# A GNN kernel whose degree histogram is laid out as 64 low columns by 98 spans instead of 128 by 49

## The chip, the cores and the metric

One NeuronCore of a Trainium2 chip runs the whole kernel. The metric is device time in microseconds (us) per execution. Engines are named as in the profile: PE is TensorE (PEld its weight loads), DVE is VectorE, ACT is ScalarE, POOL is GpSimd, SP is SyncE.

## What is computed

A graph of N = 6250 nodes and E = 100000 edges (src, dst), sorted by dst, with node features x of 6250x512 in float32. Cut to what matters:

```python
def reference(x, src, dst, ...):
    # layer 0: graph convolution with self loops
    deg  = segment_sum(ones, dst) + 1            # how many edges end in each node
    norm = rsqrt(deg)[src] * rsqrt(deg)[dst]
    h    = segment_sum(norm * (x @ W0)[src], dst) + b0 + t_emb @ Wt + bt
    x    = layernorm(x + h)
    # layers 1 and 2: mean over the incoming edges
    cnt  = segment_sum(ones, dst)
    h    = relu((segment_sum(x[src], dst) / max(cnt, 1)) @ Wl1.T + x @ Wr1.T + b1)
    h    = (segment_sum(h[src], dst) / max(cnt, 1)) @ Wl2.T + h @ Wr2.T + b2
    return layernorm(x + h)
```

All three layers need the number of edges that end in each node. That count is the histogram of this case.

## The kernel before, in words

**The constants.** P = 128 partitions, T = 49 tiles of 128 nodes, H = 64, WT = 98 windows of 64 nodes (two a tile), EC = 782 edges to a partition, HB = 34 edge columns to a block of the histogram, so EC / HB = 23 blocks.

**The histogram.** It is the first thing that the engines do, and nothing of the layers starts before it is done. SP loads dst into `dst_nat` (128x782, int32; L282). DVE makes from it `dst_hi` = dst >> 7 (the tile, 0 to 48; L473 and the cast L475), `dst_lo` = dst & 127 (the place in the tile; L474 and L478), and, for another purpose, `own_win` = dst >> 6 (the window, 0 to 97; L476, L479) and `next_win` of the next edge (L477, L480), from which L482 and L483 find whether the edges are sorted. POOL makes `iota_lo` (L378), in which element (v, c) is v.

Then for each block of 34 edge columns DVE writes two arrays of bfloat16 zeros and ones with one comparison each: `oh_lo`, 128 values by 34 columns (L494), and `oh_hi`, 49 values by 34 columns (L495). The column index c is the innermost, so the value index v has a step of 34 elements, 68 bytes. PE then runs 34 matmuls (L928), one for each column c: the stationary operand (the weights) is `oh_lo[:, half, :, c]`, 128 partitions by 128 columns, the moving one is `oh_hi[:, half, :, c]`, 128 partitions by 49 columns. Both are read with the step of 68 bytes. Each adds 128 edges to the counts in PSUM, `hist_ps[low, tile]` (`hist_ps` is another name for `root_ps`, which is how the profile writes it). L908 clears the bank before, and L937, a matmul of zeros, closes the sum and signals `hist_done`.

**What orders the two engines.** `oh_lo` and `oh_hi` have two halves. DVE waits on `oh_used` (L491) until PE has finished the block two before; PE waits on `oh_ready` (L926) for the block's arrays. The loop holds two blocks; the 23rd stands behind it.

**Behind the histogram.** DVE copies the counts (`cnt`, L504, 128x49), makes `rcnt` and `dinv` = 1 / sqrt(deg) (L505 to L509, with ACT), and 98 window totals by two matmuls of 64 partitions each (L942: `cnt[0:64]` is the first window of each tile, `cnt[64:128]` the second). From these come the tables that tell where windows end (L515 to L577). ACT and DVE scale x by `dinv` into `stage` (L793, L622), SP stores it as `table0` (L344), and when that is stored POOL starts the gathers (L441). SP's loads of dst rows, src rows and small weights behind `hist_done` (L316 to L327) go on beside that.

**The three layers.** POOL gathers 256 source rows a group by two indirect DMAs (L441) into a ring of 10 slots; PE adds them to the windows by matmuls with one-hot arrays (L1024), transposes a finished tile (L1007) and multiplies it by the weights (L1017); the root term is L1034. 391 groups a layer, three layers.

```python
            def one_hots(b, half):
                dve.wait_ge(S["oh_used"], b + 1)
...
                v.tensor_tensor(oh_lo[:, half, :, :], iota_lo[:, :, :], lo_b, ALU.is_equal)
                v.tensor_tensor(oh_hi[:, half, :, :], iota_lo[:, 0:T, :], hi_b,
                                ALU.is_equal).then_inc(S["oh_ready"], 1)
```

Of the kernel before, what the change touches and what calls it, by code (L numbers as in the profile page):

```python
# [5 lines left out]
def gnn_resnorm(nc, x, src, dst, t_emb, w0, b0, wt, bt, wl1t, wr1t, b1, wl2t, wr2t, b2, out):  # L6
    fp32, bf16 = mybir.dt.float32, mybir.dt.bfloat16
    i32, i16 = mybir.dt.int32, mybir.dt.int16
    ALU, ACT = mybir.AluOpType, mybir.ActivationFunctionType
# [3 lines left out]
    P = 128  # L13
    T = -(-N // P)
# [4 lines left out]
    H = P // 2  # L19
    WT = 2 * T  # L20
# [25 lines left out]
    EC = -(-E // P)  # L46
# [3 lines left out]
    HB = 34  # L50
# [6 lines left out]
    with ctx:  # L57
        def sb(name, shape, dt, scope=ctx):
            return scope.enter_context(nc.sbuf_tensor(name, shape, dt))
# [29 lines left out]
        zeros = sb("zeros", [P, P], bf16)  # L89
# [9 lines left out]

        early = ExitStack()  # L100
        dst_nat = sb("dst_nat", [P, EC], i32, early)
        dst_hi_i = sb("dst_hi_i", [P, EC], i32, early)
        dst_lo_i = sb("dst_lo_i", [P, EC], i32, early)
        dst_hi = sb("dst_hi", [P, EC], bf16, early)
        dst_lo = sb("dst_lo", [P, EC], bf16, early)
        iota_lo = sb("iota_lo", [P, P, HB], bf16, early)
        oh_lo = sb("oh_lo", [P, 2, P, HB], bf16, early)
        oh_hi = sb("oh_hi", [P, 2, T, HB], bf16, early)
        dst_next = sb("dst_next", [P, EC], i32, early)
        own_win_i = sb("own_win_i", [P, EC], i32, early)  # L110
        next_win_i = sb("next_win_i", [P, EC], i32, early)
        own_win = sb("own_win", [P, EC], bf16, early)
# [12 lines left out]
        cnt = sb("cnt", [P, T], fp32, mid)  # L125
# [60 lines left out]
        hist_ps = root_ps  # L186
# [188 lines left out]
        def _(pool):  # L375
            nc.gpsimd.memset(hpad[0:1, :], -1).then_inc(S["pad_made"], 1)
            nc.gpsimd.memset(X[:, T - 1, :], 0.0).then_inc(S["x_tail_zero"], 1)
            nc.gpsimd.iota(iota_lo[:, :, :], [[1, P], [0, HB]], base=0, channel_multiplier=0,  # L378
                           allow_small_or_imprecise_dtypes=True)
            nc.gpsimd.memset(zeros[:, :], 0.0)  # L380
            nc.gpsimd.memset(ones[:, :], 1.0)
# [73 lines left out]
        def _(dve):  # L455
            v = nc.vector
            count = [0]

            def link(ins):

                count[0] += 1
                ins.then_inc(S["chain"], 1)
                dve.wait_ge(S["chain"], count[0])
# [6 lines left out]
            dve.sem_inc(S["rstd_ready"], LAG)  # L470

            dve.wait_ge(S["dst_loaded"], 16 * 8)
            v.tensor_scalar(dst_hi_i[:, :], dst_nat[:, :], 7, None, ALU.arith_shift_right)  # L473
            link(v.tensor_scalar(dst_lo_i[:, :], dst_nat[:, :], P - 1, None, ALU.bitwise_and))  # L474
            v.tensor_copy(dst_hi[:, :], dst_hi_i[:, :])  # L475
            v.tensor_scalar(own_win_i[:, :], dst_nat[:, :], 6, None, ALU.arith_shift_right)  # L476
            v.tensor_scalar(next_win_i[:, :], dst_next[:, :], 6, None, ALU.arith_shift_right)  # L477
            link(v.tensor_copy(dst_lo[:, :], dst_lo_i[:, :]))  # L478
# [10 lines left out]
            def one_hots(b, half):  # L489

                dve.wait_ge(S["oh_used"], b + 1)  # L491
                lo_b = dst_lo[:, bass.ds(b * HB, HB)].unsqueeze(1).to_broadcast([P, P, HB])
                hi_b = dst_hi[:, bass.ds(b * HB, HB)].unsqueeze(1).to_broadcast([P, T, HB])
                v.tensor_tensor(oh_lo[:, half, :, :], iota_lo[:, :, :], lo_b, ALU.is_equal)  # L494
                v.tensor_tensor(oh_hi[:, half, :, :], iota_lo[:, 0:T, :], hi_b,  # L495
                                ALU.is_equal).then_inc(S["oh_ready"], 1)

            with dve.Fori(0, EC // HB - 1, 2) as b:
                one_hots(b, 0)
                one_hots(b + 1, 1)  # L500
            one_hots(EC // HB - 1, 0)
            dve.wait_ge(S["hist_done"], 1)
            dve.wait_ge(S["edges_copied"], 6 * 16)
            link(v.tensor_copy(cnt[:, :], hist_ps[:, 0:T]))  # L504
            link(v.tensor_scalar(rcnt[:, :], cnt[:, :], 1.0, None, ALU.max))  # L505
            v.tensor_scalar(dinv[:, :], cnt[:, :], 1.0, None, ALU.add).then_inc(S["deg_made"], 1)
            link(v.reciprocal(rcnt[:, :], rcnt[:, :]))
# [108 lines left out]
            for n, (first, many) in enumerate(TWOS):  # L616
                b = first // BT
                if b >= 2 and first % BT == 0:
                    dve.wait_ge((S["stage_stored0"], S["stage_stored1"])[b % 2], 16 * PAIRS * (b // 2))
                if many == 2:  # L620
                    t = first + 1
# [281 lines left out]
        def _(pe):  # L903
            mm = nc.tensor.matmul

            def clear(bank, cols):

                return mm(bank[:, 0:cols], zeros[:, :], zeros[:, 0:1].to_broadcast([P, cols]), start=True, stop=False,  # L908
                          skip_group_check=True)
# [9 lines left out]
            pe.wait_ge(S["consts_made"], 2)  # L919
            pe.wait_ge(S["order_read"], 1)  # L920
            mm(aggT_ps[0:1, 0:1], fall_sum[:, :], ones[:, 0:1], start=True, stop=True).then_inc(S["order_ps"], 1)
            clear(hist_ps, T)

            def count(b, half):

                pe.wait_ge(S["oh_ready"], b + 1)  # L926
                for c in range(HB):
                    last = mm(hist_ps[:, 0:T], oh_lo[:, half, :, c], oh_hi[:, half, :, c], start=False, stop=False,  # L928
                              skip_group_check=True)
                last.then_inc(S["oh_used"], 1)  # L930

            with pe.Fori(0, EC // HB - 1, 2) as b:
                count(b, 0)
                count(b + 1, 1)
            count(EC // HB - 1, 0)

            mm(hist_ps[:, 0:T], zeros[:, :], zeros[:, 0:T], start=False, stop=True,  # L937
               skip_group_check=True).then_inc(S["hist_done"], 1)

            pe.wait_ge(S["deg_made"], 1)  # L940
# [31 lines left out]
            for rows, banks, done in ((src_f, tmp_ps[0:2], "src_ps"), (drow_f, tmp_ps[2:4], "dst_ps")):  # L972
                for q in range(QC):
                    last = nc.tensor.transpose(banks[q // 4][:, q % 4 * CQ:(q % 4 + 1) * CQ], rows[0:CQ, q, :],
                                               ident[0:CQ, 0:CQ])
# [133 lines left out]
def build(nc, arrays):  # L1109
    args = [nc.dram_tensor(f"in_{n}", arrays[f"in_{n}"].shape, mybir.dt.from_np(arrays[f"in_{n}"].dtype),  # L1110
                           kind="ExternalInput").ap() for n in _INS]
    out = nc.dram_tensor("out_0", arrays["in_x"].shape, mybir.dt.float32, kind="ExternalOutput").ap()
    gnn_resnorm(nc, *args, out)
# [14 lines left out]
```

## Time and profile before

| | |
|---|---|
| median of 3 runs | 3257.88 us (3256.55 to 3260.6) |
| the profiled execution | 3249.74 us |
| its span on the core | 3248.0 us |
| mean granted TensorE clock | 0.932 of full |
| busy: PE, PEld | 2715.4 us (84%), 920.1 us (28%) |
| busy: DVE, ACT, POOL | 1075.9 us (33%), 493.5 us (15%), 2240.1 us (69%) |
| histogram, first matmul to last | 18.16 to 96.56 us |
| first gather | 140.91 us |

The profile is of one execution. The time of an execution is its span and some 1.7 us around it. Busy time of PE is the union of its matmuls, whose ends are modelled; "idle before" names what an engine waited for. A row's mean is of one instruction. In a timeline a row merges neighbouring instructions of one kind; it gives the start, the time from that start to the end of the last, and how many there are.

### The profile page before, as it was taken

To read this page: it belongs to the slowest core of one execution; us is meant where nothing else is said; L and a number is where in the kernel's file an instruction comes from. 1 tells how busy PE (TensorE), PEld (TensorE's weight loads), DVE (VectorE), ACT (ScalarE), POOL (GpSimd) and SP (SyncE) were. 2 spreads that over 40 slices of the span, in tenths; PEclk is the share of its full clock that TensorE was granted. 3 is DMA by queue.
4 is the path that set the end of the run, shared out by engine and by line. 5 is a ranking of instruction groups with operands and counts; after the bars stand their busy time and mean duration, and the time that the engine had idled before them with its cause. 6 is when DMAs were issued, how large, how long until landed. Compare 5 with 4: busy or idle time off the path is not lost.

```text
span 3248.0 us, 48588 instructions
## 1 busy us (share of the span) xinstructions
PE 2715.4 (84%) x9664; PEld 920.1 (28%) x9665; DVE 1075.9 (33%) x2322; ACT 493.5 (15%) x1044; POOL 2240.1 (69%) x2367
## 2 busy tenths in 40 slices
PE   7466677778898989899889888988888988888897
PEld 6211111222222233333322222223333333222222
DVE  8401122334454521122222233332222333333443
ACT  0200001111122210111111111120001111112222
POOL 1277777777777657777777777737777777777663
PEclk9766888999999999999999999999999999999999
DMA  6777777777777667778888887758777777777773
GB/s 197 255 210 209 209 216 220 223 222 228 225 229 229 197 189 242 235 236 252 247 244 248 248 248 240 243 175 249 238 227 230 240 232 230 234 219 229 207 212 120
DMA packets 255898, 729.72 MB, mean 225 GB/s; under 512 B 50026, under 2 KB 51596, under 8 KB 255842
## 3 DMA queue, kind: packets, MB, share of 16 engines
q0 software_dynamic: 187680, 615.14, 64.6%
q1 hardware_dynamic: 52528, 85.56, 7.4%
q10 hardware_dynamic: 15666, 28.72, 2.6%
q8 instruction: 12, 0.20, 0.0%
q14 instruction: 12, 0.10, 0.0%
HBM read 676.34 MB, written 53.71 MB: 225 GB/s over the span
## 4 chain that ended last, share of the span: by engine, by line
PE 59%; issue 15%; POOL 10%; DMA 7%; DVE 4%; DVEq 3%; ACT 2%; SPq 0%; POOLq 0%; ACTq 0%
PE sum_ps L1024 32%; PE prod_ps L1017 13%; PE root_ps L1034 10%; POOL raw L441 10%; DMA raw<-table,idx_ring 5%; PE aggT_ps L1007 2%; PE root_ps L928 1%; PE selfT_ps L1048 1%; ACT half_sum L825 1%; DMA raw<-rows,idx_ring 1%; DVE oh L720 1%; DVEq L254 1%; DVE X L641 1%; DVE X L644 1%; DMA selfbuf<-rows 1%
## 5 line engine op out<-in xcount | busy, mean ns | idle before, releaser
L441 POOL DMA_INDIRECT raw<-rows,idx_ring x1564 | 1487.1, 951 | 594.1 <-issue 501.0
L1024 PE MATMUL sum_ps<-raw,oh 128*64 128x512 f32 x4692 | 1228.1, 646 | 338.9 <-DMA raw<-table,idx_ring 153.5
L441 POOL DMA_INDIRECT raw<-table,idx_ring x782 | 742.7, 950 | 286.5 <-issue 259.5
L1017 PE MATMUL prod_ps<-W,aggT 128*128 128x512 f32 x1176 | 619.7, 652 | 28.2 <-issue 25.7
L1024 PEld LDWEIGHTS sum_ps<-raw,oh 128*64 128x64 f32 x4692 | 305.5, 142 | 1057.7 <-issue 1054.2
L671 DVE TENSOR_TENSOR agg<-sum_ps,half_sum 64x512 f32<-64x512 f32 x294 | 200.9, 683 | 1115.4 <-ACT half_sum L825 1115.2
L1034 PE MATMUL root_ps<-W,selfT 128*128 128x512 f32 x800 | 396.9, 642 | 103.4 <-issue 45.1
L825 ACT ACTIVATE half_sum<-sum_ps 64x512 f32<-64x512 f32 x294 | 174.4, 593 | 1231.5 <-PE sum_ps L1024 1231.5
L1017 PEld LDWEIGHTS prod_ps<-W,aggT 128*128 128x128 f32 x1176 | 213.6, 202 | 449.5 <-issue 449.5
L1024 PE MATMUL sum_ps<-raw,oh_next 128*64 128x512 f32 x1176 | 319.8, 622 | 9.4 <-DVE agg L671 9.4
L720 DVE TENSOR_TENSOR oh<-iota_ps,dst_rel 128x640 f32<-128x640 f32 x237 | 194.6, 821 | 382.5 <-PE sum_ps L1024 353.6
L1034 PEld LDWEIGHTS root_ps<-W,selfT 128*128 128x128 f32 x800 | 153.8, 202 | 333.7 <-issue 311.4
L699 DVE TENSOR_SCALAR oh_next<-iota_row,win_base,dst_end 128x64 f32<-128x64 bf16 x588 | 164.1, 334 | 44.3 <-DVE dst_end L696 18.7
L696 DVE CAST dst_end<-dst_tab 128x2 f32 x294 | 58.3, 198 | 361.7 <-issue 217.7
L836 ACT ACTIVATE selfT<-selfT_ps 128x512 f32<-128x512 f32 x100 | 59.7, 597 | 722.5 <-PE selfT_ps L1048 722.5
L815 ACT ACTIVATE aggT<-aggT_ps 128x512 f32<-128x512 f32 x147 | 87.9, 598 | 470.6 <-PE aggT_ps L1007 470.6
L1024 PEld LDWEIGHTS sum_ps<-raw,oh_next 128*64 128x64 f32 x1176 | 59.0, 136 | 243.2 <-issue 243.2
L1007 PE MATMUL aggT_ps<-ident,agg 128*128 128x128 f32 x588 | 96.8, 287 | 0.0
L1007 PEld LDWEIGHTS aggT_ps<-ident,agg 128*128 128x128 f32 x588 | 61.9, 141 | 120.7 <-issue 100.4
L928 PE MATMUL root_ps<-oh_hi,oh_lo 128*128 128x49 bf16 x782 | 75.0, 269 | 7.0 <-DVE oh_hi L495 6.8
L928 PEld LDWEIGHTS root_ps<-oh_hi,oh_lo 128*128 128x128 bf16 x782 | 70.3, 142 | 11.7 <-DVE oh_hi L495 11.7
L843 ACT ACTIVATE junk<-X,sums 128x512 f32 (+1 forms) x98 | 69.8, 712 | 6.5 <-DVE sums L663 6.5
(140 smaller groups left out, 761.9 us busy)
## 6 DMA issues: line engine op xcount, KB each, us to landing
selfbuf<-rows ACTq DMA_DIRECT2D x103, 256.0 KB
raw<-rows,idx_ring POOLq DMA_INDIRECT x1564, 3.8
rows<-X SPq DMA_DIRECT2D x49, 256.0 KB, 3.8
rows<-hbuf SPq DMA_DIRECT2D x49, 256.0 KB
X<-rows SPq DMA_DIRECT2D x49, 256.0 KB
raw<-table,idx_ring POOLq DMA_INDIRECT x782, 3.7
X<-in_x SPq DMA_DIRECT2D x6, 2048.0 KB
out<-X SPq DMA_DIRECT2D x48, 256.0 KB
```

Of the source, the lines that this page charges most:

```text
L441: nc.gpsimd.indirect_dma_start(out=raw[:, n, j, :], out_offset=None, in_=tables[L][:, :], in_offset=bass.IndirectOffsetOnAxis(ap=idx_ring[ ...
L671: v.tensor_tensor(agg[h * H:(h + 1) * H, :], sum_ps[0:H, :], half_sum[:, :], ALU.add).then_inc(S["agg_ready"], 1)
L699: made = v.tensor_scalar(oh_next[:, j, :], iota_row[:, 0:H], win_base[:, bass.ds(w1, 1)], dst_end[:, j:j + 1], ALU.add, ALU.is_equal)
L720: v.tensor_tensor(oh[:, which * HR:(which + 1) * HR, :, :].rearrange("p n j e -> p (n j) e"), iota_ps[:, 0:H].unsqueeze(1).to_broadcast([P ...
L815: a.activation(aggT[:, :], aggT_ps[:, :], ACT.Copy).then_inc(S["aggT_ready"], 1)
L825: a.activation(half_sum[:, :], sum_ps[H:P, :], ACT.Copy).then_inc(S["half_taken"], 1)
L843: a.activation(junk[:, :], tile_of_x(t1), ACT.Square, bias=column(sums, t1), accum_out=column(sqsum, t1)).then_inc(S["squares_made"], 1)
L928: last = mm(hist_ps[:, 0:T], oh_lo[:, half, :, c], oh_hi[:, half, :, c], start=False, stop=False, skip_group_check=True)
L1007: last = nc.tensor.transpose(aggT_ps[:, k * P:(k + 1) * P], agg[:, k * P:(k + 1) * P], ident[:, :])
L1017: last = mm(product(L, t1), aggT[:, k * P:(k + 1) * P], W[:, 0, k, :], start=(k == 0), stop=(k == KD - 1))
L1024: return mm(sum_ps[j * H:(j + 1) * H, :], of[:, j, :], raw[:, n, j, :], start=fresh, stop=False, skip_group_check=True)
L1034: last = mm(out_ps, xT[:, k * P:(k + 1) * P], W[:, n, k, :], start=(k == 0), stop=(k == KD - 1))
```

## The change

The node number is split at bit 6 in place of bit 7. `dst_lo` = dst & 63 has 64 values, and the other half of the split is `own_win` = dst >> 6 with 98 values, which DVE has anyway, so `dst_hi_i` and `dst_hi` go. The stationary operand is now 128 partitions by 64 columns and the moving one 128 by 98; the counts stand in PSUM as `hist_ps[0:64, 98]`. `cnt` keeps its layout: it is put together by two copies, one for even windows into partitions 0 to 63 and one for odd windows into 64 to 127, each reading every second column. The number of blocks, of matmuls (782) and the waits stay as they were.

```diff
-        dst_hi_i = sb("dst_hi_i", [P, EC], i32, early)
-        dst_hi = sb("dst_hi", [P, EC], bf16, early)
-        iota_lo = sb("iota_lo", [P, P, HB], bf16, early)
-        oh_lo = sb("oh_lo", [P, 2, P, HB], bf16, early)
-        oh_hi = sb("oh_hi", [P, 2, T, HB], bf16, early)
+        iota_lo = sb("iota_lo", [P, WT, HB], bf16, early)
+        oh_lo = sb("oh_lo", [P, 2, H, HB], bf16, early)
+        oh_hi = sb("oh_hi", [P, 2, WT, HB], bf16, early)
...
-            nc.gpsimd.iota(iota_lo[:, :, :], [[1, P], [0, HB]], base=0, channel_multiplier=0,
+            nc.gpsimd.iota(iota_lo[:, :, :], [[1, WT], [0, HB]], base=0, channel_multiplier=0,
...
-            v.tensor_scalar(dst_hi_i[:, :], dst_nat[:, :], 7, None, ALU.arith_shift_right)
-            link(v.tensor_scalar(dst_lo_i[:, :], dst_nat[:, :], P - 1, None, ALU.bitwise_and))
-            v.tensor_copy(dst_hi[:, :], dst_hi_i[:, :])
+            link(v.tensor_scalar(dst_lo_i[:, :], dst_nat[:, :], H - 1, None, ALU.bitwise_and))
...
-                lo_b = dst_lo[:, bass.ds(b * HB, HB)].unsqueeze(1).to_broadcast([P, P, HB])
-                hi_b = dst_hi[:, bass.ds(b * HB, HB)].unsqueeze(1).to_broadcast([P, T, HB])
-                v.tensor_tensor(oh_lo[:, half, :, :], iota_lo[:, :, :], lo_b, ALU.is_equal)
-                v.tensor_tensor(oh_hi[:, half, :, :], iota_lo[:, 0:T, :], hi_b,
+                lo_b = dst_lo[:, bass.ds(b * HB, HB)].unsqueeze(1).to_broadcast([P, H, HB])
+                win_b = own_win[:, bass.ds(b * HB, HB)].unsqueeze(1).to_broadcast([P, WT, HB])
+                v.tensor_tensor(oh_lo[:, half, :, :], iota_lo[:, 0:H, :], lo_b, ALU.is_equal)
+                v.tensor_tensor(oh_hi[:, half, :, :], iota_lo[:, :, :], win_b,
                                 ALU.is_equal).then_inc(S["oh_ready"], 1)
...
-            link(v.tensor_copy(cnt[:, :], hist_ps[:, 0:T]))
+            by_half = hist_ps[0:H, 0:WT].rearrange("p (t h) -> p t h", h=2)
+            v.tensor_copy(cnt[0:H, :], by_half[:, :, 0])
+            link(v.tensor_copy(cnt[H:P, :], by_half[:, :, 1]))
...
-            clear(hist_ps, T)
+            clear(hist_ps, WT)
...
-                    last = mm(hist_ps[:, 0:T], oh_lo[:, half, :, c], oh_hi[:, half, :, c], start=False, stop=False,
+                    last = mm(hist_ps[0:H, 0:WT], oh_lo[:, half, :, c], oh_hi[:, half, :, c], start=False, stop=False,
                               skip_group_check=True)
...
-            mm(hist_ps[:, 0:T], zeros[:, :], zeros[:, 0:T], start=False, stop=True,
+            mm(hist_ps[:, 0:WT], zeros[:, :], zeros[:, 0:WT], start=False, stop=True,
                skip_group_check=True).then_inc(S["hist_done"], 1)
```

## Rows read from the trace of the kernel before

**Rows 1.** Start of the page: span, busy time, granted clock in 40 slices.

```profile
span 3248.0 us, 48588 instructions
PE 2715.4 (84%) x9664; PEld 920.1 (28%) x9665; DVE 1075.9 (33%) x2322; ACT 493.5 (15%) x1044; POOL 2240.1 (69%) x2367
PEclk9766888999999999999999999999999999999999
```

**Rows 2.** Chain of waits in the histogram, one turn: start us, us, what.

```profile
31.84 3.27 PE root_ps L928 x34
35.41 2.17 issue
37.58 1.03 DVE oh_hi L495
```

**Rows 3.** Timeline: start us, us, engine, line, count, idle before; DVE and POOL ahead.

```profile
1.72 6.09 POOL L378 IOTA iota_lo<- 128x4352 bf16 x1
6.77 1.47 DVE L473 TENSOR_SCALAR dst_hi_i<-dst_nat 128x782 int32<-128x782 int32 x1 [6.63 <-DMA dst_next<-hpad]
8.16 0.78 DVE L474 TENSOR_SCALAR dst_lo_i<-dst_nat 128x782 int32<-128x782 int32 x1
8.98 0.58 DVE L475 CAST dst_hi<-dst_hi_i 128x782 bf16<-128x782 int32 x1
9.48 0.65 DVE L476 TENSOR_SCALAR own_win_i<-dst_nat 128x782 int32<-128x782 int32 x1
```

**Rows 4.** Timeline, DVE in the histogram: the first block and two neighbouring ones.

```profile
14.74 2.43 DVE L494 TENSOR_TENSOR oh_lo<-iota_lo,dst_lo 128x4352 bf16<-128x4352 bf16 x1 [0.19 <-issue]
28.41 2.43 DVE L494 TENSOR_TENSOR oh_lo<-iota_lo,dst_lo 128x4352 bf16<-128x4352 bf16 x1 [0.22 <-PE root_ps L928]
30.76 1.02 DVE L495 TENSOR_TENSOR oh_hi<-iota_lo,dst_hi 128x1666 bf16<-128x1666 bf16 x1
31.69 2.42 DVE L494 TENSOR_TENSOR oh_lo<-iota_lo,dst_lo 128x4352 bf16<-128x4352 bf16 x1
```

**Rows 5.** Timeline, PE in the histogram: two blocks, and the last one.

```profile
31.84 6.52 PE L928 MATMUL root_ps<-oh_hi,oh_lo 128*128 128x49 bf16 x68 [0.34 <-DVE oh_hi L495]
38.66 6.54 PE L928 MATMUL root_ps<-oh_hi,oh_lo 128*128 128x49 bf16 x68 [0.31 <-DVE oh_hi L495]
93.25 3.27 PE L928 MATMUL root_ps<-oh_hi,oh_lo 128*128 128x49 bf16 x34 [0.22 <-DVE oh_hi L495]
```

**Rows 6.** Lines L928 and L908: duration ns min/median/max, first and last start, forms.

```profile
L928 PEld LDWEIGHTS root_ps<-oh_hi,oh_lo x782: 136/142/171, 18.2 to 96.2; 128*128 128x128 bf16 x196
L928 PE MATMUL root_ps<-oh_hi,oh_lo x782: 262/269/292, 18.2 to 96.3; 128*128 128x49 bf16 x196
L908 PE MATMUL root_ps<-zeros x1: 221/221/221, 14.2 to 14.2; 128*128 128x49 bf16 x1
L908 PE MATMUL sum_ps<-zeros x1: 609/609/609, 124.3 to 124.3; 128*128 128x512 bf16 x1
```

**Rows 7.** Timeline, narrow windows: PEld and PE at the first block, PEld and PE at the end.

```profile
18.15 0.14 PEld L928 LDWEIGHTS root_ps<-oh_hi,oh_lo 128*128 128x128 bf16 x1 [3.84 <-DVE oh_hi L495]
18.15 0.20 PEld L928 LDWEIGHTS root_ps<-oh_hi,oh_lo 128*128 128x128 bf16 x2 [3.84 <-DVE oh_hi L495]
18.16 0.28 PE L928 MATMUL root_ps<-oh_hi,oh_lo 128*128 128x49 bf16 x1 [3.72 <-DVE oh_hi L495]
18.16 0.38 PE L928 MATMUL root_ps<-oh_hi,oh_lo 128*128 128x49 bf16 x2 [3.72 <-DVE oh_hi L495]
96.34 0.22 PE L937 MATMUL root_ps<-zeros 128*128 128x49 bf16 x1
```

**Rows 8.** Timeline behind the histogram, to the first gather.

```profile
96.59 0.21 DVE L504 COPY cnt<-root_ps 128x49 f32<-128x49 f32 x1 [3.40 <-PE root_ps L937]
...
98.04 0.20 DVE L512 COPY n_w<-prod_ps 128x49 f32<-128x49 f32 x1
98.15 0.20 DVE L513 COPY n_w<-prod_ps 128x49 f32<-128x49 f32 x1
98.16 5.00 ACT L793 ACTIVATE stage<-X,dinv 128x512 f32<-128x512 f32 x8 [0.62 <-DVE dinv L509]
...
140.91 1.10 POOL L441 DMA_INDIRECT raw<-table,idx_ring  x1 [43.95 <-issue]
```

**Rows 9.** Windows: length, busy (x) of PE, PEld, DVE, ACT, POOL, PEclk, DMA share, GB/s.

```profile
40.00:50.00 10.00, 9.68 (x104) 9.06 (x102) 9.61 (x7) 0.00 (x0) 0.00 (x0) 1.00 1.05 387
120.00:140.00 20.00, 3.92 (x16) 2.63 (x15) 6.91 (x14) 9.43 (x18) 0.00 (x0) 0.50 0.97 376
```

## The prediction

> **What bounds the kernel now.** I read the page first [rows 1]: PE is busy for 84% of 3248.0 us, POOL for 69%, DVE for 33%. The change touches none of the three layers, only the histogram ahead of them. So the second view is the timeline behind the histogram [rows 8]: the copy of the counts starts at 96.59 us, 0.03 us behind the last matmul, ACT scales x from 98.16, and the first gather is issued at 140.91. All of that hangs on the counts, and no engine does work of the layers before. A microsecond in the histogram is therefore a microsecond at the end, gain or loss; I move everything behind 96.56 us rigidly and take 1 for the factor.
>
> Inside the histogram the chain of waits [rows 2] alternates: PE's 34 matmuls 3.27 us, then DVE's two comparisons (the row "issue" of 2.17 us is its oh_lo), then PE again. DVE needs 2.35 us from the start of oh_lo to that of oh_hi and 0.93 from there to the next oh_lo [rows 4], so 3.28 a block if it never waits. PE takes 6.82 us for two blocks, 6.52 of them busy [rows 5]. The ring of two halves closes as DVE 3.37 + PE 3.27 + two hand-overs of 0.06 and 0.13 = 6.83 us for two blocks. **The two engines are matched within 4%: whichever the change slows sets the pace.**
>
> **DVE's part.** A block's comparisons fall from 4352 + 1666 = 6018 elements to 2176 + 3332 = 5508. The slope between the two forms is (2350 - 930) / (4352 - 1666) = 0.53 ns an element and some 0.05 us a piece [rows 4]. So oh_lo takes 1.20 us, oh_hi 1.81, together 3.01 in place of 3.28: 0.27 us less a block. Both stay what they are in kind, bfloat16 with the same broadcast.
>
> **PE's part, on which all hangs.** The number of matmuls stays 782; each loads 64 weight columns instead of 128, and streams 98 columns instead of 49. Now they stand (6520 - 269) / 67 = 93 ns apart over two blocks, (3270 - 269) / 33 = 91 within one [rows 5, 6]. Does the load or the stream make these 91 ns? Three readings say the stream.
>
> First, the durations. Two matmuls of zeros, whose moving operand is not spread over 68 byte steps, took 221 ns for 49 columns and 609 for 512 [rows 6]: 0.84 ns a column and 180 fixed. That slope is one column a cycle at the low level, 1.2 GHz; the windows give 0.50 for the stretch of the 609 ns one and 1.00 in the histogram [rows 9], while the 221 ns at 14.2 us lies on the low level's line if the fixed part is the same, so I take durations rather than that column here. The histogram's matmul with the same shape took 269 (least 262): 89 ns over the fixed part, 82 at least. So 49 strided columns stream in 82 to 89 ns, 1.67 to 1.82 ns each, twice a dense column, and this is as long as the spacing.
>
> Second, the block's start. The first load ends at 18.29, the second at 18.35, 0.06 later; yet the second matmul ends 0.10 behind the first, 18.54 against 18.44 [rows 7]. The second matmul had its weights early and still came a full spacing later.
>
> Third, the end: the matmul L937 starts at 96.34, 0.09 behind the last counting one, though its own weights are dense zeros [rows 7]. A lighter load did not shorten the spacing.
>
> If the stream is the limit, 98 columns take 98 x 1.67 = 164 ns at least, and 2 x 91 = 182 at most. From the load I expect no limit: two loads of 128 ended 0.06 us apart [rows 7], and even at 1.8 ns a column 64 of them take 115 ns, behind the stream. I take 175 ns for the spacing, between the ends because some of the 91 ns may be a fixed few. PE then needs 34 x 0.175 = 5.95 us a block against DVE's 3.01: PE alone sets the pace, and DVE's gain is hidden entirely, but for the first block.
>
> Here the Trainium skill speaks against the change: SBUF — State Buffer, the note on cachelines in the section on the DMA port swizzle, has an operand read at full rate only if successive accesses fall into the same line of 16 bytes, and a penalty for each access that crosses to a new one. By that rule every column of both operands pays at a step of 68 bytes, and the side that streams grows from 49 such accesses to 98; the trace agrees, with 269 ns against 221 for the same 49 columns.
>
> **The sum**, against the profiled execution:
> - dst_hi_i and dst_hi go: 8.16 - 6.77 = 1.39 and 9.48 - 8.98 = 0.50 us [rows 3]. The first was slow (its twin at 9.48 took 0.65), and it ended just after POOL's iota, which shrinks to 98/128 of 6.09 us and is over at 6.4, before DVE starts. So I take -1.9; if the slowness passes to the next instruction, -1.1.
> - the first block's arrays: -0.3 [rows 4].
> - PE: now 96.34 - 18.16 = 78.2 us from the first counting matmul to L937. Afterwards 782 x 0.175 = 136.9. Difference +58.7.
> - L504 becomes two copies. The second, of 64 partitions, starts about 0.1 behind the first, as L513 does behind L512; bounds 0 and one more copy of 0.21 [rows 8]: +0.1. The clear and the closing matmul have 49 columns more, 0.04 us each, the clear hidden.
>
> Sum: -1.9 - 0.3 + 58.7 + 0.1 = +56.6 us. The profiled 3249.74 becomes 3306.3. It lies 8.1 us under the median of the three runs, 3257.88; the same difference on the median gives **3314.5 us**. With 164 ns: 782 x 0.164 = 128.2, so +48.0, 3305.9. With 182 ns: 142.3, so +62.1, 3320.0 (+62.9 with the slow prologue). The layers have changes of their own from run to run; the shown runs span 4 us.
>
> **The rivals.**
> 1. *The load is the limit and the spacing shrinks: faster.* Place: PE's 782 pairs. If the 91 ns belong to the load of 128 columns, 64 take between 46 ns (proportional) and 83 (both operands' columns added, 162 against 177). Then DVE or the ring sets the pace. With 46, DVE's 3.01 a block: 23 x 3.01 + 34 x 0.046 = 70.8 us from DVE's first comparison to the end, now 96.34 - 14.74 = 81.6; that is -10.8 and with the prologue -12.6, 3245.3. With 83 the ring is 3.10 + 0.19 + 34 x 0.083 + 0.18 = 6.29 for two blocks, 11.5 of them and the start 75.3: -6.3 and -1.8, 3249.8. It decides if the spacing falls below 91 ns; for it speaks that the recorded load of 142 ns starts with each matmul, against it the three readings above.
> The rule that would bring this about is in TensorE: Matmul & The Clock Gate, section "Back-to-back issue gap": N / 2.4 + 2.5 ns for N columns; an estimate by that page is 43 ns for 98 columns. By it PE would wait for DVE throughout and the result would be rival 1's. The trace disagrees already for 49 columns, where it gives 23 and the row shows 91.
> 2. *The spacing stays near 91 ns,* because it is a fixed time of a pair, or because a busier stream lifts the clock from the low level and halves the strided column as well. Ring: 3.10 + 0.19 + 3.26 = 6.55 for two blocks, in all 78.4 us against 81.6, -3.2 and -1.8: 3252.9, within 0.2%. For it: the spacing did not change from the first block to the last; against it: the 48 ns between strided and dense durations.
> 3. *Only half of the 91 ns scales:* spacing 136 ns, 106.4 us, +28.2 - 2.1, 3284.0.
> 4. *The change hurts in another place too:* the halved array or the load without a way to hide behind a stream. If load and stream added up, 115 + 175 = 290 ns would be possible, +146 us. The rows show load and matmul overlapped throughout, so I give it little.
>
> **How the numbers follow.** My forecast, a stream of 164 to 182 ns, has 0.78, rival 1 0.10, rival 2 0.05, rival 3 0.05, rival 4 0.02. A measurement of this kernel can tell about 0.2% (6.5 us) from no change. Faster: rival 1, of which a small part falls under 6.5 us: 0.1. Same: rival 2: 0.05. Slower: the rest, 0.85. The forecast's own range is 3305 to 3321. The range that holds the time 8 times in 10 takes rival 3 in and some us above for a contention of load and stream over the 91 ns row: 3284 to 3326.
>
> **What would show it.** In the profile afterwards, L928's counterpart should stand 175 ns apart, 34 of them 5.95 us, with a recorded duration near 180 + 170 = 350 ns; PE should never wait for oh_hi after the first block, and DVE should wait some 2.9 us a block on oh_used. oh_lo should be near 1.2 us and oh_hi near 1.8; the first comparison should start near 12.8 us, the copy of the counts near 153, the first gather near 197. A spacing under 100 ns, or idle time of PE on oh_hi in every block, would make the forecast wrong; so would a change of the layers' length by more than a few us.

## The result, and the profile after

| | before | changed |
|---|---|---|
| median of the runs | 3257.22 us (4 runs, 3253.26 to 3260.6) | 3312.03 us (4 runs, 3307.6 to 3318.74) |
| ratio | | 1.0176, 95% interval 1.0159 to 1.0194 |
| profiled execution, span | 3249.74, 3248.0 us | 3315.45, 3313.7 us |
| first comparison of DVE | 14.74 us | 12.59 us |
| copy of the counts starts | 96.59 us | 151.91 us |
| first gather | 140.91 us | 196.43 us |

The change makes the kernel 54.8 us slower by the medians, against 57.3 forecast from a median of 3257.22 (56.6 from the profile, on 3257.88). In the two profiled executions it is 65.7 us, 55.5 of them ahead of the first gather; the rest is 10.2 us in layers that no edit touched, which vary from one execution to the next. In the first and the last of the three groups of runs below the layers took some 770 us longer, in the kernel before as well (medians 4029.93 and 4021.72 us in place of 3257), while the histogram's times agreed to 0.2 us, so those groups serve for their traces and their ratios are wide. The line numbers of the changed kernel are 2 to 4 lower: L490 and L491 are the comparisons, L926 the counting matmul, L935 the closing one.

The chain of waits of the changed kernel, in the stretch from 60 to 80 us, has one piece where before it alternated between PE and DVE [rows 2]:

```profile
59.88 20.13 PE root_ps L926 x116
```

The timeline of the changed kernel: DVE's first block, one later, PE, and what follows (start us, us, engine, line, count, idle before).

```profile
12.59 1.29 DVE L490 TENSOR_TENSOR oh_lo<-iota_lo,dst_lo 128x2176 bf16<-128x2176 bf16 x1 [0.19 <-issue]
13.80 1.89 DVE L491 TENSOR_TENSOR oh_hi<-iota_lo,own_win 128x3332 bf16<-128x3332 bf16 x1
...
15.74 16.55 PE L926 MATMUL root_ps<-oh_hi,oh_lo 128*64 128x98 bf16 x94 [3.41 <-DVE oh_hi L491]
...
27.92 1.29 DVE L490 TENSOR_TENSOR oh_lo<-iota_lo,dst_lo 128x2176 bf16<-128x2176 bf16 x1 [2.80 <-PE root_ps L926]
...
151.61 0.26 PE L935 MATMUL root_ps<-zeros 128*128 128x98 bf16 x1
151.91 0.20 DVE L501 COPY cnt<-root_ps 64x49 f32<-64x49 f32 x1 [8.90 <-PE root_ps L935]
152.13 0.20 DVE L502 COPY cnt<-root_ps 64x49 f32<-64x49 f32 x1
...
196.43 1.10 POOL L439 DMA_INDIRECT raw<-table,idx_ring  x1 [44.16 <-issue]
```

PE's matmuls run without a break: (16.55 - 0.35) / 93 = 174 ns apart, in place of 91 to 93 [rows 5]. DVE, matched with PE before [rows 4], now waits 2.80 us in each block. The view of the matmul's own line shows the durations and both sides of the wait:

```profile
L926 PEld LDWEIGHTS root_ps<-oh_hi,oh_lo x782: 187/192/208, 15.7 to 151.2; 128*64 128x64 bf16 x196
L926 PE MATMUL root_ps<-oh_hi,oh_lo x782: 352/352/417, 15.7 to 151.3; 128*64 128x98 bf16 x196
its engine sat idle before it (us, times) until:
  DVE oh_hi L491: 7.0, 2
who waited for it (us, times):
  DVE oh_lo L490: 59.3, 21
```

352 ns against 269 [rows 6] is 83 more for 49 columns more, 1.7 ns a column. The load now takes 192 ns where it took 142, although it has half the columns.

### The profile page after: what moved, and what is told of

Same layout as the page of the kernel before. It is cut to its first block, busy times and chain, and to the rows that moved or that the text cites. A ratio compares the mean times of both kernels' runs of the same rounds, so it can differ in the third digit from the quotient of the medians.

```text
span 3313.7 us, 48587 instructions
## 1 busy us (share of the span) xinstructions
PE 2786.1 (84%) x9664; PEld 988.7 (30%) x9665; DVE 1068.5 (32%) x2321; ACT 493.4 (15%) x1044; POOL 2238.4 (68%) x2367
## 4 chain that ended last, share of the span: by engine, by line
PE 63%; issue 13%; POOL 9%; DMA 7%; DVE 3%; DVEq 2%; ACT 1%; SPq 0%; POOLq 0%; ACTq 0%
PE sum_ps L1022 32%; PE prod_ps L1015 13%; PE root_ps L1032 10%; POOL raw L439 9%; DMA raw<-table,idx_ring 5%; PE root_ps L926 4%; PE aggT_ps L1005 2%; PE selfT_ps L1046 1%; ACT half_sum L823 1%; DMA raw<-rows,idx_ring 1%; DVE oh L718 1%; DMA selfbuf<-rows 1%; DVEq L252 1%; DVE X L642 1%; DVE X L639 1%
## 5 line engine op out<-in xcount | busy, mean ns | idle before, releaser
L926 PE MATMUL root_ps<-oh_hi,oh_lo 128*64 128x98 bf16 x782 | 135.9, 353 | 3.4 <-DVE oh_hi L491 3.4
L926 PEld LDWEIGHTS root_ps<-oh_hi,oh_lo 128*64 128x64 bf16 x782 | 135.6, 192 | 3.6 <-DVE oh_hi L491 3.6
```

Of the source, the lines that this page charges most:

```text
L926: last = mm(hist_ps[0:H, 0:WT], oh_lo[:, half, :, c], oh_hi[:, half, :, c], start=False, stop=False, skip_group_check=True)
```

## The experiments

The theory on trial is the forecast's: the moving operand's strided columns cost about 1.7 ns each and set the spacing. The rivals are that the load sets it, that both reads share one rate, that the PE clock does, and that the number of columns costs and not their step. A ratio is the run's time over that of the kernel before in the same group, with its 95% interval. The first, the second and the run with the two removed instructions are single executions and are read for their traces alone.

**Shapes and steps by themselves.** Behind the histogram of the changed kernel 19 series of 24 matmuls, each on a line of its own, for example

```diff
             count(EC // HB - 1, 0)
...
+            for c in range(24): mm(prod_ps[0:128, 0:49], lo_st[:, 0:128, c], hi_st[:, 0:49, c], start=True, stop=True, skip_group_check=True)
+            for c in range(24): mm(prod_ps[0:128, 0:49], lo_st[:, 0:128, c], hi_f[:, c:c + 49], start=True, stop=True, skip_group_check=True)
+            for c in range(24): mm(prod_ps[0:128, 0:49], lo_f[:, c:c + 128], hi_st[:, 0:49, c], start=True, stop=True, skip_group_check=True)
...
```

where `_st` is the array with 68 bytes between values and `_f` the same memory read densely.

> The changed kernel with 19 series of 24 extra matmuls each behind the histogram, on lines of their own, into a bank that nobody reads. Stream theory (a strided moving column costs about 1.7 ns, a dense one 0.84): spacing 91 ns for 128 weight columns strided by 49 moving strided and also when the weights are dense or only 64; 173 for 98 strided moving columns whatever the weights (128 or 64, strided or dense); about 113 for the swapped form, 98 by 64; about 85 for 98 dense moving columns. With steps of 4, 8, 16 and 32 bytes in the moving operand: about 85 at 4 bytes, and 173 somewhere between 16 and 32. Load theory: the spacing follows the weights, 91 for every 128 strided, 45 to 60 for 64, and dense weights shorten it. Contention theory (both reads share one rate): spacing follows the sum of strided columns, 177 columns 91 ns, so 49 strided moving with dense weights falls to about 40, and 128 by 98 strided rises above 128 by 49 by less than 49 x 1.7.

The timeline of PE in this run (stationary columns stand behind the `*`, moving ones behind the x):

```profile
151.62 2.37 PE L939 MATMUL prod_ps<-oh_hi,oh_lo 128*128 128x49 bf16 x24
153.82 1.56 PE L940 MATMUL prod_ps<-oh_hi,oh_lo 128*128 128x49 bf16 x24
155.20 2.24 PE L941 MATMUL prod_ps<-oh_hi,oh_lo 128*128 128x49 bf16 x24
157.26 1.18 PE L942 MATMUL prod_ps<-oh_hi,oh_lo 128*128 128x49 bf16 x24
158.37 4.41 PE L943 MATMUL prod_ps<-oh_hi,oh_lo 128*64 128x98 bf16 x24
162.60 2.83 PE L944 MATMUL prod_ps<-oh_hi,oh_lo 128*64 128x98 bf16 x24
165.23 4.34 PE L945 MATMUL prod_ps<-oh_hi,oh_lo 128*64 128x98 bf16 x24
169.39 2.14 PE L946 MATMUL prod_ps<-oh_hi,oh_lo 128*64 128x98 bf16 x24
171.46 4.44 PE L947 MATMUL prod_ps<-oh_hi,oh_lo 128*128 128x98 bf16 x24
175.83 2.96 PE L948 MATMUL prod_ps<-oh_hi,oh_lo 128*64 128x49 bf16 x24
178.72 4.38 PE L949 MATMUL prod_ps<-oh_lo,oh_hi 128*98 128x64 bf16 x24
183.03 2.17 PE L950 MATMUL prod_ps<-oh_hi,oh_lo 128*64 128x98 bf16 x24
184.99 2.35 PE L951 MATMUL prod_ps<-oh_hi,oh_lo 128*64 128x98 bf16 x24
187.16 4.38 PE L952 MATMUL prod_ps<-oh_hi,oh_lo 128*64 128x98 bf16 x24
191.37 4.47 PE L953 MATMUL prod_ps<-oh_hi,oh_lo 128*64 128x98 bf16 x24
195.77 1.58 PE L954 MATMUL prod_ps<-oh_hi,oh_lo 128*128 128x16 bf16 x24
197.20 0.80 PE L955 MATMUL prod_ps<-oh_hi,oh_lo 128*128 128x16 bf16 x24
197.93 2.86 PE L956 MATMUL prod_ps<-oh_hi,oh_lo 128*64 128x16 bf16 x24
200.65 1.43 PE L957 MATMUL prod_ps<-oh_hi,oh_lo 128*64 128x16 bf16 x24
```

A series' spacing is its time less the duration of one matmul, over 23; for L939 (2.37 - 0.27) / 23 = 91 ns, for L945 (4.34 - 0.35) / 23 = 173. Worked out so:

| line | stationary | moving | spacing, ns |
|---|---|---|---|
| L939 | 128, 68 bytes | 49, 68 bytes | 91 |
| L940 | 128, 68 bytes | 49, dense | 58 |
| L941 | 128, dense | 49, 68 bytes | 86 |
| L942 | 128, dense | 49, dense | 42 |
| L943 | 64, 68 bytes | 98, 68 bytes | 176 |
| L944 | 64, 68 bytes | 98, dense | 110 |
| L945 | 64, dense | 98, 68 bytes | 173 |
| L946 | 64, dense | 98, dense | 81 |
| L947 | 128, 68 bytes | 98, 68 bytes | 177 |
| L948 | 64, 68 bytes | 49, 68 bytes | 116 |
| L949 | 98, 68 bytes | 64, 68 bytes | 175 |
| L950 to L953 | 64, dense | 98, step of 4, 8, 16, 32 bytes | 82, 90, 175, 179 |
| L954, L955 | 128, 68 bytes; 128, dense | 16, dense | 60, 27 |
| L956, L957 | 64, 68 bytes; 64, dense | 16, dense | 113, 53 |

Three things follow. The load theory falls: dense weights change 91 to 86, a dense moving operand to 58. The contention theory falls too: with dense weights it wanted 40, and 128 by 98, both strided (L947), was to rise above 128 by 49 by less than 49 x 1.7 = 83 ns and rises by 86. And it is the step and not the count: the same 98 columns cost 82 ns at 4 bytes, 90 at 8 and 175 at 16. The Trainium skill's note on cachelines (SBUF — State Buffer, the section on the DMA port swizzle) asks for two accesses to a line of 16 bytes for the full rate, and these four series agree, with the edge between 8 and 16 bytes. The same note has 8 bf16, 16 bytes, as how far one may stride for free; read as a step, that does not agree with the 175 ns.

Two expectations missed. The swapped form, 98 by 64, was to take 113 and took 175; 64 by 49 was to take 91 and took 116. Both are loads. A load of 64 strided columns needs 110 to 116 ns (L944, L948) and one of 98 needs 175, 1.8 ns a column, while one of 128 strided columns is done in 58 to 60 (L940, L954). That only a load of all 128 columns of a type other than float32 goes the fast way is a rule of the Trainium skill, TensorE: Matmul & The Clock Gate, section "Weight-path perf modes"; the trace agrees as to the number of columns, and no run here loads float32 for comparison. So the load of the change is the slower one too: its 110 ns were hidden behind the 173 of the stream.

**Step or clock.** Series of 60 as above, each behind 48 dense matmuls of 512 columns.

> The changed kernel with series of 60 extra matmuls, each behind 48 dense matmuls of 128 by 512 that should bring the clock to its high level. If a strided column costs PE cycles (2 a column), its spacing falls from 173 to about 85 ns for 64 by 98 and from 91 to about 45 for 128 by 49 at the high level; if it costs time in memory, 173 and 91 stay and only the dense 64 by 98 falls, from about 85 to about 45. If the recorded durations meant nothing for the level, the 98 column dense series would have the same spacing here as in the other run.

```profile
152.02 1.91 PE L939 MATMUL prod_ps<-oh_hi 128*128 128x512 bf16 x4 [0.34 <-issue]
```

```profile
157.63 4.71 PE L939 MATMUL prod_ps<-oh_hi 128*128 128x512 bf16 x21
...
163.56 10.66 PE L940 MATMUL prod_ps<-oh_hi,oh_lo 128*64 128x98 bf16 x60
...
186.67 5.59 PE L942 MATMUL prod_ps<-oh_hi,oh_lo 128*128 128x49 bf16 x60
...
204.25 2.81 PE L944 MATMUL prod_ps<-oh_hi,oh_lo 128*64 128x98 bf16 x60
```

The windows of the same run (length, busy time of PE, PEld, DVE, ACT, POOL, granted clock, DMA share, GB/s):

```profile
140.00:150.00 10.00, 10.00 (x60) 10.00 (x59) 3.02 (x2) 0.00 (x0) 0.00 (x0) 1.00 0.01 2
164.00:174.00 10.00, 10.00 (x59) 9.89 (x57) 0.00 (x0) 0.00 (x0) 0.00 (x0) 0.71 0.01 2
187.00:192.00 5.00, 5.00 (x59) 5.00 (x57) 0.00 (x0) 0.00 (x0) 0.00 (x0) 1.00 0.00 0
```

The first fence is the narrow window right behind the histogram, the second later ones of the same run. The first four dense matmuls stand (1.91 - 0.62) / 3 = 430 ns apart, 512 columns at 1.2 GHz; the later 21 stand (4.71 - 0.38) / 20 = 217, at 2.4 GHz. So PE came out of 136 us of counting, busy all the time, at the low level, though the windows give 1.00 for the histogram. The reading of durations in place of that column was right. Behind clock-lifting matmuls the dense series L944 has a spacing of 44 ns in place of 81. The strided ones keep theirs: (10.66 - 0.35) / 59 = 175 and (5.59 - 0.27) / 59 = 90. The 0.71 of the middle window has both levels in it: narrower windows give 1.00 from 164 to 168 us and 0.50 from 169 to 173, with PE busy throughout, and in each of these stretches 25 matmuls of L940 take 4.51 and 4.52 us, 173 ns apart. So a strided column does not follow the PE clock, and the rival by which a busier PE would lift the clock and halve the column falls. That the time is the memory's is what the edge between 8 and 16 bytes speaks for; the runs show it no further.

**Only the moving operand at 4 bytes.** Two edge columns stand inside the value index:

```diff
+        CI = 2
...
-        oh_hi = sb("oh_hi", [P, 2, WT, HB], bf16, early)
+        oh_hi = sb("oh_hi", [P, 2, HB // CI, WT, CI], bf16, early)
...
-                win_b = own_win[:, bass.ds(b * HB, HB)].unsqueeze(1).to_broadcast([P, WT, HB])
+                win_b = own_win[:, bass.ds(b * HB, HB)].rearrange("p (o i) -> p o i", i=CI)
+                win_b = win_b.unsqueeze(2).to_broadcast([P, HB // CI, WT, CI])
+                numbers = iota_lo[:, 0:WT, 0:CI].unsqueeze(1).to_broadcast([P, HB // CI, WT, CI])
...
-                v.tensor_tensor(oh_hi[:, half, :, :], iota_lo[:, :, :], win_b,
+                v.tensor_tensor(oh_hi[:, half, :, :, :], numbers, win_b,
                                 ALU.is_equal).then_inc(S["oh_ready"], 1)
...
-                    last = mm(hist_ps[0:H, 0:WT], oh_lo[:, half, :, c], oh_hi[:, half, :, c], start=False, stop=False,
+                    last = mm(hist_ps[0:H, 0:WT], oh_lo[:, half, :, c], oh_hi[:, half, c // CI, :, c % CI], start=False, stop=False,
                               skip_group_check=True)
```

> The changed kernel with only the moving array oh_hi laid out with a step of 4 bytes; the stationary oh_lo keeps 68 bytes. From the series: a load of 64 columns at 68 bytes is slower than one of 128 columns, 112 ns, and now sets the spacing: PE 34 x 0.112 = 3.8 us a block, above DVE's 3.01. The copy of the counts starts at 12.6 + 3.1 + 23 x 3.83 = 103.8 us, 7 us later than before, and the time is before + 7 = 3264 where before is 3257 (ratio 1.002). If only the stream mattered, spacing would be about 82 or 45 ns, DVE would pace, the copy at 84 and the time before - 12.5.

```profile
L494 DVE TENSOR_TENSOR oh_hi<-iota_lo,own_win x23: 3082/3093/3096, 13.8 to 108.1; 128x3332 bf16<-128x3332 bf16 x23
```

Copy of the counts at 115.56 us and 3276.81 us in place of 3264; ratio 1.0059 (1.0045 to 1.0074). Within a block the load did set the spacing, 113 ns (34 loads in 3.92 us, of 0.21 each), but DVE was late as well: its comparison took 3.09 us instead of 1.89, and PE waited for it 20.7 us in all. It now read the numbers in pairs 68 bytes apart, and the next run puts that right. With a small dense array of numbers for this comparison:

> The run with only the moving array at a step of 4 bytes again, with a small dense array of numbers for its comparison (98 values by 2), since there DVE read the numbers at a step of 68 bytes and took 3.09 us for oh_hi in place of 1.89. Now oh_hi is 1.89 again, and the load of 64 columns at 68 bytes sets the pace: spacing 112 ns, 3.85 us a block, copy of the counts at 12.6 + 3.1 + 23 x 3.85 = 104.3 us, 7.7 after the kernel before, time before + 8, ratio 1.0024. If the load hides, DVE paces and the copy is at 84.

The timeline of that run, DVE's first block and PE:

```profile
14.68 1.89 DVE L497 TENSOR_TENSOR oh_hi<-iota_hi,own_win 128x3332 bf16<-128x3332 bf16 x1
...
16.63 33.59 PE L932 MATMUL root_ps<-oh_hi,oh_lo 128*64 128x98 bf16 x295 [3.41 <-DVE oh_hi L497]
```

The comparison is back at 1.89 us, so the scattered read was what cost DVE 1.2 us. The matmuls stand (33.59 - 0.31) / 294 = 113 ns apart, the copy of the counts at 105.50 us, of which 0.9 is a later start behind POOL's second iota; ratio 1.0022 (0.9993 to 1.0052), in the group with long layers. So with the stream made cheap the load is the next limit, as the series had it, and the histogram of 64 by 98 ends 8.9 us later than that of the kernel before; the interval of the time holds no change as well.

**Only the stationary operand at 4 bytes.** The same edit on `oh_lo` alone.

> The changed kernel with only the stationary array oh_lo laid out with a step of 4 bytes, the moving one at 68 bytes. Stream theory: the load is hidden behind the stream, so nothing changes: spacing 173 ns, copy of the counts at 151.9 us, time as the changed kernel's, before + 55 (ratio 1.017). Load or contention theory: spacing falls, by the sum of strided columns to 98/162 of 173 = 105 ns, copy at 98, time before + 2.

The matmul's line in this run:

```profile
L929 PEld LDWEIGHTS root_ps<-oh_hi,oh_lo x782: 128/152/153, 16.5 to 151.7; 128*64 128x64 bf16 x196
L929 PE MATMUL root_ps<-oh_hi,oh_lo x782: 351/352/359, 16.5 to 151.9; 128*64 128x98 bf16 x196
```

The load falls from 192 to 152 ns and the matmul stays at 352. The copy of the counts starts at 152.49 us; 3309.45 us, ratio 1.0159 (1.0145 to 1.0174). The spacing stays, as the stream theory says. DVE's `oh_lo` took 2.08 us in place of 1.29, since here it read its numbers in pairs 68 bytes apart; the first matmul comes 0.8 us later by it, and from there on the stream hides it.

**Both at 4 bytes, in the changed kernel.** `oh_lo`, `oh_hi` and `iota_lo` all with two edge columns innermost, `iota_lo` 98 by 2.

> The changed kernel with the one-hot arrays laid out so that two edge columns stand inside the value index: the step between values is 4 bytes instead of 68, for both operands; same numbers of elements and matmuls. Stream theory: spacing 82 to 85 ns, PE 2.9 us a block, below DVE's 3.01; if DVE keeps its rate with rows of 2 elements the histogram takes 23 x 3.01 + 2.9 = 72 us from 12.6, ends at 85 and the time is 3312 - 67 = 3245 us, 12 under before. If the number of columns and not their step is what costs, spacing stays 173 and the time 3312. If DVE falls to half its rate for rows of 2, a block takes 5.9 us and the time is again about 3312, but with PE idle.

> The changed kernel with a step of 4 bytes for both arrays, a second time, since the chip of the first time ran the layers 780 us longer. The copy of the counts starts at 83.7 us as in the first, 12.9 before that of the kernel before; if a microsecond of the histogram is one of the end, the time is before - 13, ratio 0.9960. If the layers take it back, ratio 1.0.

> The same version without the extra matmuls, on the same chip and beside the same runs of the kernel before: first gather at 128.3 us, 12.6 earlier; rigid: ratio 0.9961, time before - 12.7. If the second time's 20 us was a property of the kernel and not of the executions: ratio 0.994.

| | copy of the counts | median | ratio |
|---|---|---|---|
| first time | 83.70 us | 4023.2 (before 4029.93) | 0.9979 (0.9952 to 1.0007) |
| second | 83.88 us | 3237.61 (before 3257.57) | 0.9937 (0.9924 to 0.9950) |
| third | 83.93 us | 4010.81 (before 4021.72) | 0.9966 (0.9937 to 0.9994) |

The timeline of the second time:

```profile
60.76 1.29 DVE L498 TENSOR_TENSOR oh_lo<-iota_lo,dst_lo 128x2176 bf16<-128x2176 bf16 x1
...
60.90 1.76 PE L934 MATMUL root_ps<-oh_hi,oh_lo 128*64 128x98 bf16 x34 [1.25 <-DVE oh_hi L499]
61.96 1.89 DVE L499 TENSOR_TENSOR oh_hi<-iota_lo,own_win 128x3332 bf16<-128x3332 bf16 x1
63.76 1.29 DVE L498 TENSOR_TENSOR oh_lo<-iota_lo,dst_lo 128x2176 bf16<-128x2176 bf16 x1
```

DVE never stops and takes 3.00 us a block at its full rate; PE is done in 1.76 and waits 1.25. Here the clock does rise. In the first block the spacing is about 82 ns, which is the low level, and in this one (1.76 - 0.21) / 33 = 47, which is the high one. The histogram ends 12.7 us before that of the kernel before. The version is faster than the kernel before in the second group and, by less, in the third, while the interval of the first group holds no change.

**Both at 4 bytes, in the kernel before.**

> The kernel before (128 by 49) with the same layout, a step of 4 bytes. Stream theory: the 49 columns stream in about 41 ns, spacing then set by the load, 40 to 60 ns; DVE alone paces at 3.28 us a block: 23 x 3.28 + 2 = 77.4 us in place of 81.6, and 0.8 less ahead as POOL's iota is short: 5 us faster, about 3252. Load theory: the same if the step is what slows the load; columns-cost theory: 3257, no change. DVE at half rate: 6.4 us a block, +70 us.

> The kernel before with a step of 4 bytes for both arrays, a second time. Copy of the counts at 90.2 us as in the first, 6.4 before that of the kernel before; time before - 6.4, ratio 0.9980.

The first time the copy of the counts started at 90.16 us, ratio 0.9963 (0.9933 to 0.9993); the second at 90.31 us, 3250.37 us, ratio 0.9973 (0.9962 to 0.9984). PE takes 1.60 us for 34 matmuls of 49 columns, (1.60 - 0.22) / 33 = 42 ns apart where they stood 91, and waits 1.67 us in each block; DVE takes 3.27 us a block. So with the step out of the way the window split is worth 90.3 - 83.9 = 6.4 us in the histogram. That is the gain that was hidden in the change: 510 elements less a block, 23 x 0.27 = 6.2 us, and 0.9 for the two instructions ahead. Some 0.7 of it is lost again, and no run takes that apart.

**The two removed instructions.** `dst_hi_i` and `dst_hi` put back into the changed kernel, without readers.

> The changed kernel with the two removed instructions put back (dst_hi_i and dst_hi, whose results nobody reads): the first comparison starts where DVE's prologue then ends. My reading: the removed pair was worth 1.9 us, of which 0.8 came from POOL's longer iota. With POOL's iota short the pair costs 0.5 + 0.5 = 1.0 us: first comparison at 13.6 us instead of 12.6 (and 14.7 in the kernel before). If the slow first instruction is slow whatever POOL does, 14.0 to 14.7.

The first comparison starts at 13.66 us, `dst_hi_i` takes 0.99 and its successor starts 0.91 behind it. The pair costs 1.07 us when POOL's iota is short. Of the 2.15 us between 14.74 and 12.59 another 0.3 is an edge load that landed earlier in that profile, and 0.75 is left for the long iota [rows 3]. Other runs speak for POOL as the cause: with the second iota beside it, from 6.39 to 7.59 us, DVE's first instruction took 1.65 us; in the changed kernel, where the iota is over at 6.42 and POOL's small instructions follow, 0.94; and in both versions at 4 bytes, where POOL is done before DVE starts, 0.57.

**The same end from a shorter histogram.** 59 matmuls of zeros behind the histogram of the 4 byte version, 12.7 us.

> The changed kernel with a step of 4 bytes for both arrays, with 59 matmuls of zeros by 512 columns behind the histogram, 12.7 us at 216 ns each, so that the counts are there at 96.6 us as in the kernel before. If a microsecond ahead of the first gather is one of the end, the time is that of the kernel before, ratio 1.000. If the layers of this version are themselves some 7 us shorter, as the 20 us gained instead of 12.7 would have it, ratio 0.998.

The copy of the counts started at 96.59 us, the first gather at 141.05. Ratio 0.9984 (0.9955 to 1.0013), beside 0.9966 (0.9937 to 0.9994) for the version without them on the same chip. Both intervals hold both expectations; this one told nothing apart.

## Why the prediction was right

**The place and the factor.** Everything behind the histogram was to move rigidly. The copy of the counts moved by 55.3 us, the first gather by 55.5, the median by 54.8. That the medians come so near is in part luck, since the executions of one kernel lie up to 11 us apart. In the group with layers of the usual length the other kernels' medians moved by 19.2, 51.9 and -7.2 us for a copy that moved by 19.0, 55.9 and -6.3: a factor of 1 within some 4 us. The one that does not fit is the 4 byte version, -20.0 us for -12.7.

**The spacing.** Forecast 175 ns between 164 and 182; measured 174 in the histogram and 173 in the series. The 175 was a choice between the ends, made because some of the 91 ns might be a fixed few: 49 strided columns take 86 ns with dense weights and 98 take 173, so the stream itself has no fixed part, and the other 5 ns come with strided weights. In the sum the term 782 x 0.175 = 136.9 us measured 151.61 - 15.74 = 135.9. The duration forecast as near 350 ns was 352.

**The three readings.** All three proved good. 180 ns fixed and 0.84 a dense column put 89 ns on 49 strided columns, where the series gave 86 to 91. The second load that was early, and the closing matmul whose light load bought nothing, said that the load was not the limit, and the series says the same: dense weights save 5 ns of 91, and a load of 128 strided columns can be done in 58.

**DVE.** The slope of 0.53 ns an element gave 1.20 and 1.81 us; measured 13.80 - 12.59 = 1.21 and 15.60 - 13.80 = 1.80. The gain was hidden as forecast; DVE waited 2.80 us a block for a forecast of 2.9.

**The prologue.** -1.9 forecast; the first comparison came 2.15 us earlier, 1.8 of it without the earlier load. The cause given, POOL's iota, fits the run with the two instructions put back, where the pair costs 1.07 us with the shorter iota in place of 1.89 with the long one, and so do the first instruction's 1.65 us beside a second iota and 0.57 beside an idle POOL.

**The load.** It was rightly taken to be hidden, but the 115 ns, "even at 1.8 ns a column", were a bound for the worst case and no forecast, and it is luck that 110 to 116 were measured. The reason given, two loads of 128 ended 0.06 us apart, does not carry over: 128 strided columns take 58 to 60 ns and 64 take 110 to 116. Rival 1's bounds of 46 to 83 for 64 columns were wrong throughout, by the same step from a load of 128 to one of 64. Rival 2 falls with the 174 ns, its clock part with the series at both levels as well, rival 3 (half of it scales) with the measured 83 ns for 49 columns more, rival 4 because the time is that of the stream alone: +54.8 us where load and stream added up would give +146.

**The formula of 43 ns.** The Trainium skill's formula for the spacing (TensorE: Matmul & The Clock Gate, section "Back-to-back issue gap") gives an estimate of 43 ns for 98 columns at the high level. Dense columns agree, 44 measured behind the clock-lifting matmuls, and stood 81 apart at the low level. The prediction set it aside because of the 91 ns of its row, rightly; what made the difference was the low level and, at either level, the step of 68 bytes.

## What to carry to other kernels

Ask of each matmul operand how many bytes lie between neighbouring columns, and which operand streams: from 16 bytes on a moving column took 1.8 ns here, twice the 0.8 of a dense one at the low level (98 in 175 and in 81 ns), and at 68 bytes it gained nothing from the high clock. Columns that are moved over from the stationary side make the stream longer. Putting two columns of the batch inside the value index costs nothing in the engine that writes the array, provided its own inputs stay dense. It brought the spacing from 174 to 47 ns in the changed kernel, where the clock rose as well, and from 91 to 42 in the kernel before. When two engines are matched, a saving in one is worth nothing if the same edit lengthens the other.

## What the runs showed of the hardware that was not expected

- A load of fewer columns can take longer. 64 strided columns 110 to 116 ns, 98 columns 175, 128 columns 58 to 60; with dense weights, 128 columns by 16 moving ones stood 27 ns apart and 64 by 16 stood 53.
- PE was busy without a break for 136 us of strided matmuls and its clock was at the low level at the end (430 ns for 512 columns). In the version with dense reads PE was busy 1.76 us in 3.01 and ran at the high level from about the third block on (47 ns for 98 columns). The column of the granted clock says 1.00 in both. Later in the run with lifted clock that column does fall, from 1.00 to 0.50 at 168 us, inside a series of strided matmuls with PE busy without a break.
- DVE compares 3332 elements in 1.89 us, with rows of 2 elements as well as of 34, but in 3.09 when one input comes in pairs 68 bytes apart; 2176 elements take 1.29 and 2.08 us. That is 0.36 ns an element more in both.
- DVE's first instruction, on 782 elements of int32, took 0.57 us with POOL idle, 0.94 beside POOL's small instructions, and 1.47 and 1.65 beside an iota.

Left open: why the 4 byte version gained 20.0 us (interval 16 to 25) where its histogram is 12.7 us shorter. Beside long layers the medians differed by 6.7 and 10.9 us; both intervals hold 12.7, and the first ends at 19.3, just short of 20.0. In the profiled execution of the second time the stretch from the first gather to the end took 3114.6 us, where the profiles of the kernel before, the changed one and the other three of that group have 3107.1 to 3117.3, so that trace shows no shorter layers; but it is the slowest of five executions. It was not settled whether the rest belongs to the kernel or to those executions. Open too is why the layers took 770 us longer in two of the groups.
